# Gated cross-attention with a two-of-eight expert layer: the experts on quarters of 224 rows instead of halves of 448

## The reference, cut to what matters

```
x = x + tanh(g_xattn) * xattn(layernorm(x), ctx, mask, ...)   # 16 heads of 16, 1500 keys per sequence
x = x + tanh(g_ffn)   * ffn(layernorm(x), router_gate, expert_gate_up, expert_down)

xattn: q, k, v projections; scores clipped to +-50; masked keys get exp(-50), not zero;
       delta = clip(scale, 0, 0.3) * (probs @ v @ Wo.T + bo), then a layernorm of delta with gamma, beta
ffn:   probs = softmax(h @ router.T); two best of 8 experts, their scores normalised to sum 1
       out = sum over those two experts of score * (up * silu(gate)) @ down[e],  gate_up 256 -> 2*128, down 128 -> 256
```

## Time and profile before

| what | value |
|---|---|
| median of three runs | 277.39 us (274.09 to 277.58) |
| the profiled execution's own time | 274.56 us |
| its span in the trace | 272.9 us |
| PE busy | 229.1 us (84%) |
| DVE busy | 176.3 us (65%) |
| ACT busy | 138.4 us (51%) |
| POOL busy | 56.2 us (21%) |
| mean granted clock of PE | 0.925 of 2.4 GHz |
| the chain that ended last | PE 66%, DVE 12%, issue 11% |

### The profile page before, as it was taken

How to read it: one execution, slowest core, us unless ns; L and a number is a source line. 1 busy time by engine, 2 the same in 40 slices (tenths; PEclk the granted TensorE clock), 3 DMA queues, 4 the chain that set the end, 5 groups by cost and what they waited for, 6 DMA issues and landing times.

```text
span 272.9 us, 7014 instructions
## 1 busy us (share of the span) xinstructions
PE 229.1 (84%) x2708; PEld 175.9 (64%) x2708; DVE 176.3 (65%) x422; ACT 138.4 (51%) x220; POOL 56.2 (21%) x90
## 2 busy tenths in 40 slices
PE   0879996219999999999999387999997829999994
PEld 0667785208888888888888276966664416556663
DVE  2788549701456998677659985692999850573535
ACT  3745769911555789699757632343334517101010
POOL 2470000200155332100002211033444643000000
PEclk9999999557999999999999959599999975999999
DMA  7999204660871589996991000310000002000002
GB/s 223 327 417 386 76 21 116 208 269 4 293 276 40 182 324 324 396 355 177 390 419 60 4 2 2 54 20 0 0 0 2 1 0 67 0 0 2 0 0 67
DMA packets 12868, 37.54 MB, mean 138 GB/s; under 512 B 2320, under 2 KB 10016, under 8 KB 10528
## 3 DMA queue, kind: packets, MB, share of 16 engines
q1 hardware_dynamic: 11728, 36.13, 37.1%
q10 hardware_dynamic: 1008, 0.92, 1.3%
q0 software_dynamic: 96, 0.00, 0.0%
HBM read 35.14 MB, written 0.92 MB: 132 GB/s over the span
## 4 chain that ended last, share of the span: by engine, by line
PE 66%; DVE 12%; issue 11%; DMA 3%; POOL 3%; ACT 3%; SPq 1%; DVEq 0%; POOLq 0%; ACTq 0%
PE bank L803 13%; PE bank L537 11%; PE bank L544 10%; PE bank L565 6%; PE bank L554 6%; PE bank L820 6%; PE bank L792 4%; DMA x_sb<-x_dram 3%; POOL x_sb L514 3%; PE bank L697 2%; PE bank L683 2%; PE bank L529 2%; PE bank L522 1%; PE bank L673 1%; DVE p L1147 1%
## 5 line engine op out<-in xcount | busy, mean ns | idle before, releaser
L537 PE MATMUL bank<-ctx_pair,wk 128*128 128x250 f32 x152 | 40.4, 409 | 17.6 <-issue 10.0
L906 ACT ACTIVATE p<-bank,mask_bias,mask_scale 125x896 f32<-125x896 f32 x38 | 39.7, 1095 | 27.8 <-PE bank L554 27.8
L803 PE MATMUL bank<-rowsT,gate_up 128*128 128x448 f32 x112 | 46.0, 557 | 0.0
L537 PEld LDWEIGHTS bank<-ctx_pair,wk 128*128 128x128 f32 x152 | 29.2, 202 | 23.2 <-issue 18.4
L544 PE MATMUL bank<-wv,ctx_pair 128*125 128x256 f32 x152 | 36.4, 383 | 0.0
L1147 DVE TENSOR_SCALAR p<-p 125x912 f32<-125x912 f32 x38 | 27.6, 738 | 12.1 <-ACT p L906 12.1
L803 PEld LDWEIGHTS bank<-rowsT,gate_up 128*128 128x128 f32 x112 | 21.9, 197 | 17.9 <-issue 17.2
L544 PEld LDWEIGHTS bank<-wv,ctx_pair 128*125 128x125 f32 x152 | 28.8, 190 | 4.4
L1029 ACT ACTIVATE silu<-bank 128x448 f32<-128x448 f32 x16 | 8.7, 546 | 44.9 <-PE bank L803 41.6
L820 PE MATMUL bank<-down,act 128*112 128x256 f32 x128 | 30.3, 380 | 1.3 <-DVE act L1455 1.3
L820 PEld LDWEIGHTS bank<-down,act 128*112 128x112 f32 x128 | 22.4, 177 | 9.4 <-issue 3.7
(11 more groups left out here) (163 smaller groups left out, 316.7 us busy)
## 6 DMA issues: line engine op xcount, KB each, us to landing
ctx_all<-ctx_dram SPq DMA_DIRECT2D x13, 1500.0 KB, 8.7
ctx_pair<-ctx_dram SPq DMA_DIRECT2D x38, 125.0 KB, 5.2
gate_up<-ctx_dram SPq DMA_DIRECT2D x3, 1500.0 KB, 10.9
gate_up<-gate_up_dram SPq DMA_DIRECT2D x1, 2048.0 KB, 12.8
down<-down_dram SPq DMA_DIRECT2D x1, 1024.0 KB, 14.8
num<-acc SPq DMA_DIRECT2D x16, 57.0 KB, 2.3
x_sb<-x_dram SPq DMA_DIRECT2D x2, 448.0 KB, 6.2
out_dram<-x_sb SPq DMA_DIRECT2D x4, 224.0 KB, 2.3
```

What stands on the lines that cost most here:

```text
L537: mm = nc.tensor.matmul(bank[:, K_BANK, 2 * TT * m:2 * TT * (m + 1)], wk[:, k, P * m:P * (m + 1)], tile[:, :, k, :], start=(k == 0), stop= ...
L803: mm = nc.tensor.matmul(bank[:, GU_BANK[s % 2] + g, 0:HR], gate_up[:, e, k, g, :], rowsT[:, k, HR * h:HR * (h + 1)], start=(k == 0), stop= ...
L906: nc.scalar.activation(p_tile[:, t].rearrange("t (j n) s -> t j n s", j=4)[:, :, :, 0:S], bank[0:TT, 0:4, DEN * t:DEN * (t + 1)].rearrange ...
```

## The change

- **Quarters.** A step `s` is now one expert on one chunk of 224 rows, 32 steps, chunk `c = s // 8`. `expert_in` makes gate and up side by side in one bank, four such banks in turn (the first two products use the banks that K and V used). `expert_out` is two matmuls. `silu` and `act` have four buffers of 224 instead of two of 448. The `expert_half` split is gone.
- **Routing by chunk.** `route`, the exponential, `shift_logits`, `expert_ranks` and `expert_weights` run four times on two blocks, instead of twice on four. `expert_ranks` loses three DVE steps (sum, reciprocal, product: the softmax's own normalisation).
- **Order.** PE: one loop over `s` with `expert_in(s)`, `expert_out(s - 2)` and the epilogue's products of the second half at set steps (6 to 11, 14, 15, 21, 22). DVE: one or two pieces of the epilogue between successive `gate` calls; `gate` runs up to three experts ahead in the last half. ACT and POOL follow the same steps. Chunks 0 and 1 are scaled by ACT and added by POOL, chunks 2 and 3 by DVE, as before.
- **The last pairs.** `project_out(0, 0)` and `(0, 1)` come before the V projection of pairs 15 and 16; the scores of pair 17 come before the transposes of chunk 0; `delta_parts` and `add_gains` stand ahead of `v_copy`; `shift_logits(0)` stands before the last clips.

The core of the diff (DVE's and ACT's order, and the loops that the order rows below show, are cut):

```diff
-        silu, act = sb("silu", [P, 2, HR]), sb("act", [P, 2, HR])
+        silu, act = sb("silu", [P, 4, CHUNK]), sb("act", [P, 4, CHUNK])
...
-        GU_BANK = [0, 2]
+        GU_BANK = [4, 5] + [s % 4 for s in range(4 * NE - 2)]
...
+            for s in range(2 * NE):
+                if s == 1:
+                    h_guess(1)
+                if s == 8:
                     delta_guess(2)
...
             for i in range(NOPT, NTAIL):
-                pair_kv(i)
+                pair_k(i)
+                if i == 15:
+                    pe.wait_ge(wide_out, 1)
+                if i in (15, 16):
+                    project_out(0, i - 15)
+                pair_v(i)
...
+            def expert_in(s):
+                c, e = s // NE, s % NE
...
+                if s >= 6:
+                    pe.wait_ge(act_out, s - 3)
+                if e == 0:
+                    pe.wait_ge(misc_out, USE[f"hT{c}"] + 1)
                 for g in range(2):
                     for k in range(HALVES):
+                        mm = nc.tensor.matmul(bank[:, GU_BANK[s], CHUNK * g:CHUNK * (g + 1)], gate_up[:, e, k, g, :],
+                                              rowsT[:, k, CHUNK * c:CHUNK * (c + 1)],
                                               start=(k == 0), stop=(k == HALVES - 1))
...
+            for s in range(2, 4 * NE + 2):
+                if s < 4 * NE:
+                    expert_in(s)
+                expert_out(s - 2)
+                if s == 6:
+                    h_transposes(1)
+                if s == 7:
+                    use("spread1")
+                    spread_inverse(1, 0, misc(0, 2 * DEN)).then_inc(misc_mm, 1)
+                    route(1)
...
+                if s == 14:
+                    h_transposes(2)
...
+            for s in range(2, 4 * NE):
+                gate_silu(s)
                 if s == 6:
+                    h_rows(1)
+                if s - 2 < 2 * NE:
+                    scale_expert(s - 2)
...
+                if s == 13:
+                    h_rows(2)
```

More of the change, by code:

```diff
@@ L685, in project_out, with h_transposes, route @@
                 mm.then_inc(misc_mm, 1)
[L687 to L695, removed]
+            def h_transposes(c):
+                use(f"hT{c}")
+                pe.wait_ge(h_normal, 2 * c + 2)
+                transposes(misc(0, 2 * CHUNK), c).then_inc(misc_mm, 1)
+            def route(c):
+                use(f"route{c}")
+                for t in range(2):
+                    r0 = CHUNK * c + R2 * t
                     for k in range(HALVES):
@@ L810, in expert_out @@
                 pe.wait_ge(act_out, s + 1)
[L811 to L822, removed]
+                if s == 2:
+                    pe.wait_ge(main.acc_out, 2 * NTAIL)
@@ L1470, in _ @@
+            gate(0)
+            delta_whole()
+            gate(1)
             pair_sums(NTAIL - 1)
             masked_sums(1)
-            shift_logits(0)
             expert_ranks(0)
+            gate(2)
             expert_weights(0)
-            gate(0)
+            gate(3)
+            add_gains(0, 1)
+            gate(4)
+            add_delta(0, 1)
+            gate(5)
+            h_offsets(0, 1)
             inverses(1)
-            gate(1)
+            gate(6)
             totals(1)
+            gate(7)
@@ L1497, in _ @@
-            shift_logits(1)
             gate(8)
@@ L1500, in _ @@
             expert_weights(1)
-            dve.wait_ge(h_normal, PAIRS)
-            dve.wait_ge(weight_out, 2)
-            for s in range(NE, 2 * NE):
-                if s + 1 < 2 * NE:
-                    gate(s + 1)
-                add_expert(s)
+            gate(9)
+            delta_parts(1, 0)
+            gate(10)
+            delta_whole()
+            gate(11)
+            add_gains(1, 0)
+            gate(12)
+            add_delta(1, 0)
+            delta_parts(1, 1)
+            gate(13)
+            h_offsets(1, 0)
+            gate(14)
+            delta_whole()
+            gate(15)
+            add_gains(1, 1)
+            shift_logits(2)
+            gate(16)
+            add_delta(1, 1)
+            gate(17)
+            h_offsets(1, 1)
+            expert_ranks(2)
+            expert_weights(2)
+            gate(18)
+            for s in range(2 * NE, 4 * NE):
+                add_expert(s)
+                if s + 3 < 4 * NE:
+                    gate(s + 3)
+                if s == 20:
+                    shift_logits(3)
+                if s == 21:
+                    expert_ranks(3)
+                    expert_weights(3)
 def kernel(x, ctx_2048, mask_BxS2_ik0, g_xattn, g_ffn, L0_xattn_Wq, L0_xattn_bq, L0_xattn_Wk, L0_xattn_bk,
```

313 lines of the change are left out of this document (132 added, 181 removed).

## The result

| | before | changed |
|---|---|---|
| median of 4 runs | 277.49 us (274.09 to 278.06) | 265.68 us (262.88 to 265.99) |
| the profiled execution, and its span | 274.56, 272.9 us | 265.4, 263.7 us |
| PE's mean granted clock | 0.925 | 0.939 |

The ratio is 0.9577, with a 95% interval of 0.9517 to 0.9636: **faster, by 11.8 us**. 18.4 us were forecast (277.39 to 259 us, range 252 to 268). The profiled executions lie closer together, 9.2 us.

The account below looks back on a forecast made before the run. PE's idle and low-clock time, behind DVE and POOL chains, was taken to bound the kernel. Span: 272.9 - 25.6 + 2.0 + 5.5 + 1.0 = 255.8 us; 257.5 as execution, 259 forecast as median, range 252 to 268.

Parts of the forecast that it names:

- What was lost, and where: PE's idle and low-clock time before the change: 25.6 us, 13.1 at the hand-over to the experts, 12.5 between the halves.
- Cost of the quarter products: 32 expert steps of 2.39 us, 76.3 us against 75.8, with 1 us added for 16 more boundaries; range 0.5 to 2.
- Hand-over: From pair 15's product to pair 17's, into the experts: 2 us of loss left, product of pair 17 ending near 161.
- I expect the clock to stay up: At the hand-over: PE's clock would not fall, as idle time is a third; about 5.5 us more if it did.
- First sixteen steps: Expert steps after pair 17's product: PE stalls on DVE, mostly before the third chunk's transposes, 5.5 us; bounds 1.5 to 7.
- rival 2: PE waits in the first sixteen steps lower the clock once or twice more, 3.4 to 4.1 us each: 264 to 271; chance 0.24.
- the lower bound for the stalls: PE's stalls in the first sixteen steps if POOL's adds lengthen no DVE step: 1.5 us.
- The estimate of some 20 us for all sixteen adds: Each POOL add could block one DVE step for up to an add's length, some 20 us, far outside the stall bounds.
- DVE is then as full as PE: First sixteen steps: DVE 54 us of work, PE 55, each waiting for the other; sign: DVE over 85% busy, 160 to 220.
- At no cost: Four more ACT table loads free, at worst 1 us each; fourth chunk's transposes free; last routing beside light DVE steps.
- the forecast's own case: It flows: stalls and clock as forecast, 252 to 264 us; chance 0.60.
- Rivals 3 and 4: DVE bounds the stage, nothing hidden: 271 to 283, chance 0.10; short waits keep PE at 1.2 GHz: 283 to 295, 0.06.

## Why the prediction was right, and where it was short

1. **What was lost, and where.** 25.6 us of idle and slow time, at the hand-over and between the halves. Right: the changed kernel gives back 8.4 of them and no PE work went away. The stretch of the last transposes is free, as forecast.
2. **Cost of the quarter products.** 1 us forecast, 0.2 measured.
3. **Hand-over.** 2 us forecast, 3.8 measured. Product of pair 17 forecast to end near 161, it ended at 162.1, and that in an execution that was 1.0 us ahead: 10.9 us behind the product of pair 15, where 8.8 were forecast. Idle 1.64 us against 1.3. Who was late was wrong: not ACT's sums (its rows were ready at 153.4) but the misc bank, which PE gets back with DVE's `fix_raw` at 153.9. "I expect the clock to stay up" failed: it fell, for 1.7 us (5.5 were priced for that).
4. **First sixteen steps, the mis-sized term.** 5.5 us, with 7 as the worst; 13.3 measured. Idle time alone was 8.6: 2.89 (forecast 1), 0.78 (1.5), 4.58 (up to 4.4), 0.35. The clock added 4.7, of which I had priced none in the sum. That was rival 2, and it came: two falls, which took 1.7 and 3.0 us where 3.4 to 4.1 each were priced. The mechanism I named, DVE's chain lengthened by POOL's adds, was right: a chain of 17 us was forecast and 16.9 measured, and with the adds cut short the profiled execution takes 255.4 us, where the sum with the lower bound for the stalls gives 253.5 (1.5 for 5.5). The steps were others than I had named: `delta_whole` ran at its quiet length, and four steps (`half_var`, `delta_rstd`, `fix_neg`, `finite`) bring 4.1 us. What I missed was that the chain to the second chunk's transposes is lengthened as well: its offsets come 17.4 us behind `gate(0)`, where 12.5 were forecast (2.89 us of stall; 14.2 and 0.65 with the adds cut short). The estimate of some 20 us for all sixteen adds was twice what came, 9.6 us over eleven steps. And the 12.2 us that I took for POOL's 16 adds are ten instructions of POOL, guesses among them; the 16 adds take 21.0 us in the kernel before.
5. **"DVE is then as full as PE".** Half wrong. It was busy 48.2 of 65 us, no more than before (the earlier trace rows has 47.9), and 45.8 of the 60 from 160 to 220, 76% where over 85% was to be the sign. It took 14 us of adds on top without harm. Its idle time lies in waits, and the stalls of PE come from long things in front of short urgent ones and from steps that POOL lengthens, as the short adds show.
6. **At no cost**: table loads (266.07 without them), fourth transposes, last routing. All right.
7. **The sum.** Span forecast 255.8, measured 263.7: 9.7 us more lost, 1.0 us ahead in front, 0.8 less for the products. The measured time lies within the range, but above 264, where the forecast's own case ended: it is the second case, given 0.24, that came. Two things brought the number nearer that the mechanism has no part in: the 1.0 us in front, and the 1.5 us added for the medians, of which 0.3 came (the profiled execution was forecast at 257.5 and took 265.4). Rivals 3 and 4 did not come.

## What to carry to other kernels

An engine that nobody waits for can still set the pace: look for instructions of the bounding chain that take longer than the same ones elsewhere, and for what another engine did at that moment. Where a long GpSimd instruction on SBUF runs beside a chain of VectorE, cut it into short ones, even if its total grows. When a stall is moved or covered, ask which wait is next on the same engine: two reorderings that each gave 2 to 3 us gave at most 1 together, with a new wait of 3.29 us further on. With that gate moved as well and the adds short, no wait behind the hand-over is over 1.06 us; how much of this is the gate's was not tried by itself.

## What the hardware did that I had not expected

- VectorE's delays hit instructions with one input and tiny ones too: a copy-sized step on 112x2 elements took 1.23 us instead of 0.17, not only the two-input steps that I had priced.
- The length of a wait does not tell whether the clock falls. Eleven of the kernels here, the changed one among them, wait 1.62 to 1.64 us before the first transposes. In nine the clock fell within 3 us (in one of these with a second wait, of 1.78 us, between); in two, the adds cut short and the copies for exponentials, it stayed up. With the adds cut short it fell near 180 us behind waits of 0.65 and 0.71 us and stayed up behind 1.57; with the extra matmuls it stayed up behind 2.33; in the kernel before it stayed up behind 1.78 near 208.
- Extra matmuls whose result nobody reads kept the clock at 1.00 from 145 to 235 us in one execution, and gave back 4.1 of 6.4 us there.
- Here a table load costs ScalarE just its 1.28 us: the exponential starts 0.02 us behind its end.

```profile
221.73 1.28 ACT L942 ACT_TABLE_LOAD   x1
223.03 0.21 ACT L942 ACTIVATE probs<-logits 112x16 f32<-112x16 f32 x1
```
